# Tridiagonalising with the unscaled column: Householder steps reordered in an eigendecomposition kernel

## The reference

```
h = relu(layernorm(x));  x = x + L0(h)
h = relu(layernorm(x));  x = x + L1(h)

L0: deg = row sum + column sum - diagonal
    L_norm = D^-1/2 (diag(deg) - A) D^-1/2
    _, U = eigh(L_norm)
    agg = U^T h;  out = relu(agg W1 + b1) W2 + b2;  return U out
L1: two graph convolutions with adj, then LSTMs over windows of
    1, 2, 3 and 4 nodes, the last state written back
```

## Time and profile before

| | |
|---|---|
| median of three runs | 1360.0 us |
| profiled execution | 1349.57 us, span 1347.7 us |
| setup, to the first step | 0 to 8.4 us |
| tridiagonalisation | 8.4 to 342.8 us |
| eigenvalues and vectors | 343 to 497 us |
| L0 and L1 products | 497 to 1347.7 us |
| busy, share of the span | PE 93%, DVE 74%, ACT 68%, POOL 25% |

### The profile page before, as it was taken

One profiled execution on the slowest core, in us unless ns is written; L12 is line 12 of the kernel. 1 busy time (PEld: TensorE's weight loads), 2 busy tenths in 40 slices (PEclk: granted clock), 3 DMA queues, 4 the chain that ended last, 5 costly groups with the idle time before them and its releaser, 6 DMA issues.

```text
span 1347.7 us, 28362 instructions
## 1 busy us (share of the span) xinstructions
PE 1255.6 (93%) x8489; PEld 1124.5 (83%) x8489; DVE 991.2 (74%) x4880; ACT 917.3 (68%) x3438; POOL 331.7 (25%) x1205
## 2 busy tenths in 40 slices
PE   8889999999776379999999999999999999999997
PEld 7778888888665368788989989989989889899897
DVE  9999999999999977766774565655645655645645
ACT  4677777777599302267957858768579588578575
POOL 0288888888886010000110000000000000000000
PEclk9999999999789679999999999999999999999999
DMA  9500000000000003300010000100100100100001
GB/s 265 128 2 2 1 2 2 2 2 2 1 1 1 0 1 95 94 1 1 1 31 0 16 16 0 31 0 0 31 0 0 31 0 0 31 0 16 17 1 33
DMA packets 43642, 28.99 MB, mean 22 GB/s; under 512 B 1520, under 2 KB 39440, under 8 KB 43536
## 3 DMA queue, kind: packets, MB, share of 16 engines
q1 hardware_dynamic: 43536, 27.81, 7.6%
HBM read 19.42 MB, written 8.39 MB: 21 GB/s over the span
## 4 chain that ended last, share of the span: by engine, by line
PE 70%; DVE 20%; ACT 3%; issue 2%; ACTq 0%; DVEq 0%
PE bank L894 14%; PE bank L884 11%; PE bank L889 9%; PE bank L897 8%; PE bank L674 7%; PE bank L814 2%; PE bank L866 2%; PE bank L687 2%; PE bank L858 2%; PE bank L822 2%; PE bank L681 2%; PE bank L852 2%; PE bank L829 2%; PE bank L837 2%; ACT BIG L615 1%
## 5 line engine op out<-in xcount | busy, mean ns | idle before, releaser
L615 ACT ACTIVATE BIG<-bank,bias 128x128 f32<-128x128 f32 (+2 forms) x544 | 226.8, 417 | 161.6 <-PE bank L897 102.1
L894 PE MATMUL bank<-spare,wT 128*128 128x256 f32 (+2 forms) x1408 | 311.3, 321 | 0.0
L615 ACT ACTIVATE PV<-bank,bias 128x256 f32<-128x256 f32 (+2 forms) x704 | 301.6, 431 | 0.0
L894 PEld LDWEIGHTS bank<-spare,wT 128*128 128x128 f32 x1408 | 234.8, 191 | 13.2
L884 PE MATMUL bank<-spare,wT 128*128 128x128 f32 (+2 forms) x1088 | 226.3, 319 | 4.1 <-DVE spare L1610 2.7
L1596 DVE TENSOR_TENSOR BIG<-BIG,PV 128x128 f32<-128x128 f32 (+2 forms) x192 | 63.0, 328 | 207.5 <-ACT BIG L615 207.4
L674 PE MATMUL bank<-ones 128*128 128x128 f32 x1350 | 213.6, 291 | 1.1 <-POOL ones L313 1.1
L884 PEld LDWEIGHTS bank<-spare,wT 128*128 128x128 f32 x1088 | 169.5, 191 | 19.2 <-DVE spare L1610 6.1
L674 PEld LDWEIGHTS bank<-ones 128*128 128x128 f32 x1350 | 174.7, 195 | 1.1 <-POOL ones L313 1.1
L897 PE MATMUL bank<-spare,wT 128*128 128x128 f32 (+2 forms) x768 | 169.7, 303 | 0.0
L889 PE MATMUL bank<-spare,wT 128*128 128x128 f32 (+2 forms) x768 | 141.7, 307 | 3.7 <-DVE spare L1608 1.2
(11 more groups left out here) (478 smaller groups left out, 2670.5 us busy)
## 6 DMA issues: line engine op xcount, KB each, us to landing
spare<-in_x SPq DMA_DIRECT2D x32, 256.0 KB, 3.9
out<-X SPq DMA_DIRECT2D x32, 256.0 KB, 2.4
spare<-in_L_gnn_Wih SPq DMA_DIRECT2D x4, 256.0 KB, 4.5
spare<-in_L_gnn_Whh SPq DMA_DIRECT2D x4, 256.0 KB, 4.4
W<-in_L_gnn_W SPq DMA_DIRECT2D x2, 64.0 KB, 3.1
Wg<-in_L_gnn_Wg SPq DMA_DIRECT2D x2, 64.0 KB, 2.6
adj<-in_adj SPq DMA_DIRECT2D x1, 64.0 KB, 1.8
X<-in_x SPq DMA_DIRECT2D x4, 0.5 KB, 17.6
```

The lines of the kernel that those rows point to most:

```text
L615: last = nc.scalar.activation(gate_out[q][i][:, 0:T], gate(i, q, T), ACT.Tanh if q == GATE_G else ACT.Sigmoid, bias=bias[:, at:at + 1])
L894: last = nc.tensor.matmul(gate(i, q, T), wT[:, 0, p - 1, q * D:(q + 1) * D], xt, start=True, stop=(j == 0))
```

## The change

The reflector's scaled form is no longer computed before the product with A. With the column x unscaled, y = A x is multiplied at once, and u, its norm and the products with it are put together afterwards from x, y and A's column. `alpha` is the reciprocal of the signed norm, `eta` that of u's leading element, both kept for all steps in `invB`. Columns have a tiny constant added (`nudge`, 1e-10), which POOL makes at the start. The signs of stored quantities are turned.

The loop's part of the diff in short form: an arrow names the semaphore that an instruction raises, and VectorE's instructions stand as the arithmetic they do, one instruction for each assignment.

```diff
 # ScalarE, per step
-  two_sigma = Sqrt(4 x.x); half_x = Abs(x_t)/2; ST = Copy(x.x)
-  ACOL; row copy; eB = Identity(sign, scale=two_sigma); x_statistics (3 ops) once
+  act.wait_ge(s_ready, k + 1)
+  nc.scalar.activation(minus_sign(k), banks[7][:, 0:1], ACT.Sign)
+  nc.scalar.activation(sigma(k), banks[7][:, 1:2], ACT.Sqrt)
+  act.wait_ge(xb_ready, 2 * k + 1)
+  nc.scalar.activation(u_row(k)[:, t + 1:N], banks[0][:, t + 1:N], ACT.Copy)
+  act.wait_ge(hv, at_hv(k, MINUS_S))
+  nc.scalar.activation(S_(UC), ident[:, t:t + 1], ACT.Identity, bias=column(k), scale=rowsB[:, k:k + 1])
+  act.wait_ge(a_ready, k + 1)
+  nc.scalar.activation(S_(ACOL), A[:, t:t + 1], ACT.Copy, scale=below[:, t:t + 1])
+  statistic(2 * k)
+  act.wait_ge(xb_ready, 2 * k + 2); act.wait_ge(hv, at_hv(k, ETA))
+  nc.scalar.activation(eta_row[:, t + 1:N], banks[3][:, t + 1:N], ACT.Copy, scale=eta[:, t:t + 1])
+  statistic(2 * k + 1)
 # TensorE, per step
   pe.wait_ge(x_ready, k + 1)
   2-column product -> s_ready
-  row product; keep_clock(1); wait u_ready, a_ready; u row x A; A x u column; keep_clock(4)
+  nc.tensor.matmul(banks[0][:, 0:N], x_wide, ident[:, 0:N])   -> xb_ready
+  pe.wait_ge(taken, taken_by(k - 1, ETA_ROW))
+  nc.tensor.matmul(banks[3][:, 0:N], x_wide, minus_ident[:])  -> xb_ready
+  pe.wait_ge(a_ready, k + 1)
+  nc.tensor.matmul(banks[2][:, 0:N], x_wide, A[:])            -> yrow_ready
+  nc.tensor.matmul(banks[4][:, 0:1], A[:], x_c)               -> ycol_ready
+  pe.wait_ge(taken, taken_by(k, COL_U))
+  nc.tensor.matmul(banks[1][:, 0:N], S_(UC).to_broadcast([N, N]), A[:])  -> p_ready
+  idle(256)                        # one product of ones with 256 columns
 # VectorE, per step: 19 instructions (L1003 to L1057) replaced by 17
+  wait sigma_ready
+  minus_s = minus_sign * sigma;  minus_ut = minus_sign * sigma + x_t
+  alpha = 1 / minus_s;  eta = 1 / minus_ut;  XA = XM * alpha;  AM = below * alpha;  HX = XA * eta
+  wait taken (ROW), yrow_ready;  uyB = sum(y row * u row)       # wide
+  HXA = HX * alpha;  wait ycol_ready;  YA = y * AM + nudge
+  column(t) = HXA * uyB + YA       -> x_ready
+  wait p_ready;  Z = alpha * uyB + p_t;  wait taken (COLUMN);  W = YA + ACOL
+  A = p row * HX + A                                            # wide
+  V = HX * Z + W;  XM = column(t) * minus_below
+  wait taken (ETA_ROW);  A = eta_row * V + A  -> a_ready        # wide
```

More of the change, by code:

```diff
@@ L674, in keep_clock, with idle @@
                     nc.tensor.matmul(spot, ones[:], ones[:], start=True, stop=True)
+            def idle(columns):
+                if columns > 0:
+                    nc.tensor.matmul(banks[5][:, 0:columns], ones[:], ones[:, 0:1].to_broadcast([N, columns]),
+                                     start=True, stop=True)
             def householder(k):
+                t = k + 1
+                from_t = slice(t, N)
+                x_c = column(k)
+                x_wide = x_c.to_broadcast([N, N])
@@ new lines, in reflector @@
+                n_s = step(V.tensor_tensor(minus_s, minus_sign(k), sigma(k), ALU.mult))
+                n_ut = step(V.scalar_tensor_tensor(out=minus_ut, in0=minus_sign(k), scalar=sigma(k), in1=x_t,
+                                                   op0=ALU.mult, op1=ALU.add))
+                dve.wait_ge(hv, n_s)
+                n_al = step(V.reciprocal(alpha[:, t:t + 1], minus_s))
+                dve.wait_ge(hv, n_ut)
+                n_eta = step(V.reciprocal(eta[:, t:t + 1], minus_ut))
+                if not last:
+                    dve.wait_ge(hv, n_al)
+                    n_xa = step(V.tensor_tensor(S(XA), S(XM), alpha[:, t:t + 1], ALU.mult))
+                    n_am = step(V.tensor_tensor(S(AM), below[:, t:t + 1], alpha[:, t:t + 1], ALU.mult))
+                    dve.wait_ge(hv, n_xa)
+                    n_hx = step(V.tensor_tensor(S(HX), S(XA), eta[:, t:t + 1], ALU.mult))
+                    dve.wait_ge(taken, taken_by(k, ROW))
@@ new lines, in reflector @@
+                dve.wait_ge(yrow_ready, k + 2)
+                n_uy = step(V.tensor_tensor_reduce(out=wB[:, t:N], in0=banks[2][:, t:N], in1=u_row(k)[:, t:N], scale=1.0,
+                                                   scalar=0.0, op0=ALU.mult, op1=ALU.add, accum_out=uyB[:, t:t + 1]))
+                if last:
+                    return n_uy, None
+                dve.wait_ge(hv, n_hx)
+                step(V.tensor_tensor(S(HXA), S(HX), alpha[:, t:t + 1], ALU.mult))
+                dve.wait_ge(ycol_ready, k + 1)
@@ new lines, in diagonal @@
+            def diagonal(out, r, row, own):
+                h.last(dve)
+                op(V.tensor_tensor(row, alpha[r], uyB[r], ALU.mult))
+                op(V.tensor_tensor(own, wB[r], eta[r], ALU.mult))
+                op(V.tensor_tensor(row, row, own, ALU.subtract))
+                op(V.tensor_tensor(out, row, alpha[r], ALU.mult))
+            below_of(0)
+            for k in range(LEAF):
+                update(k, *reflector(k))
+            dve.wait_ge(taken, 1)
+            op(V.tensor_copy(d16[:, 0:1], dB[LP, 0:1]))
@@ L1073, in _ @@
             for k in range(LEAF, STEPS):
-                before = householder(k, before)
-            dve.wait_ge(e_ready, STEPS)
-            dve.wait_ge(a_ready, N)
+                n_uy, n_ya = reflector(k)
+                if k + 1 < STEPS:
+                    update(k, n_uy, n_ya)
             def go(ins):
```

278 lines of the change are left out of this document (137 added, 141 removed).

## The result

| | before | after |
|---|---|---|
| median | 1359.95 us | 1314.01 us |
| lowest and highest of four runs | 1351.77 to 1366.04 | 1313.11 to 1314.66 |
| profiled execution, its span | 1349.57, 1347.7 us | 1313.11, 1311.1 us |

The ratio is 0.9665, 95% interval 0.9614 to 0.9717: 46 us by the medians, 36.5 us by the two profiled executions. The profiled execution of before is not one of its four runs.

What follows compares the result with a forecast made beforehand. VectorE's in-order queue, taken as without holes, bounds the loop. 0.39 x 127 + 1 (diagonal) - 1 (X late) = 50, less 5 of POOL wait: 45 us off the 1360.0 median gives 1315 us, range 1302 to 1336.

Steps and rivals of the forecast that it cites:

- The step: Tridiagonalisation loop: a step falls from 2.63 to 2.24 us, saving 0.39 x 127 = 50 us.
- T+0.79: Start of A's second update, 0.79 us after T, the start of the VectorE instruction that writes the step's column.
- Just in time: In the loop step, the row A x is ready at S+0.65 (S: reflector start), exactly when VectorE reaches the dot product.
- ring: Loop path from A's second update through row product to dot product; row priced at T+1.65, equal to VectorE's queue.
- Rival B: Loop: ScalarE's or TensorE's queue late in every step, 2.40 us a step, gain 29, 1331 us; chance 0.20.
- The start and the diagonal: Once-only terms: X late for the statistics costs 1 us; dropping the diagonal's TensorE trip at step 16 gains 1.
- POOL: Leaf sweeps beside and behind the loop: end at about 435 us, VectorE's diagonal line then waits 5 us (bounds 0, 18).
- rival C: Behind the loop: POOL much later, an 18 us wait, gain 32, 1328 us; chance 0.07.
- A: Behind the loop: POOL is not last, gain 50 to 52, 1309 us; chance 0.15.
- D: Loop: Sign and Sqrt in different ScalarE tables, two loads a step, about 1635 us; chance 0.05.
- E: Loop: TensorE's clock falls to 1.2 GHz, steps up to 3.4 to 3.6 us, 1460 us; chance 0.04.
- Its own signs of being wrong: Four: table loads in the loop; clock below 1.00 before 290 us; VectorE idle before the reflector; POOL done well before diagonal.

Runs made afterwards that it cites:

- the XM run: Changed kernel with the masked-column instruction moved from before A's second update to behind it: 1315.5 us.
- the added copy: Changed kernel with one more one-column VectorE copy per step, right ahead of the dot product: 1313.6 us, 0.6 above the unedited kernel beside it.
- 17 sweeps: Changed kernel with 17 instead of 16 leaf QR sweeps on POOL: 1320.3 us; the same edit in the kernel before: ratio 0.9996.
- the dummies that removed it: Kernel before with one more 128 x 128 dummy product in each step from step 96 on: 1351.7 us.
- the kernel of 1432.7 us: Changed kernel with all four row products of a step narrowed to the live columns: 1432.7 us.

## Why the prediction was right, and where it was not

1. **The step.** Predicted 2.24 us, measured 2.33 as a mean, so 12 of the 50 us did not come. The structure was right in that all engines fit, A x comes just when the dot product asks for it, and the row product is the long link. It was wrong in what sets the step: the prediction took VectorE's queue to be without holes, and it has 2.6 us of them in 60. Two terms of the path through the row product were too small. I let A's second update start at T+0.79; it starts at T+0.86, because the dependent instruction comes 0.31 behind V, not 0.25 (the XM run shows the same 0.32 with nothing between them). And I let a reader on VectorE start 0.04 behind the end of a product, from the row of ScalarE (L493) in the earlier trace rows; L1059 starts 0.15 behind L733. With 0.03 more between the update and the product, and the part from the dot product to the next column 0.05 shorter than priced, that is 2.18 + 0.07 + 0.11 + 0.03 - 0.05 = 2.34, the step shown. "Just in time" was the place to look twice: where queue and ring are priced as equal, any error in the ring shows in full and one in the queue doesn't (the added copy: 0.6 us).
2. **Rival B** had 2.40 by late queues of ScalarE or TensorE. The size lies as near to B as to the forecast; the cause isn't B's. In the step shown TensorE and ScalarE both wait 0.38 us for VectorE's column and its product, and in every step of the profile but the one at half clock TensorE's first product (L726) starts 0.27 to 0.32 us behind the column: its queue is not late.
3. **The statistics** beside VectorE's steps: nothing, as predicted (0.1%, within the error).
4. **The start and the diagonal.** ScalarE waits 0.84 us for X and VectorE 0.21 for that: under the 1 us taken. At the leaf break a step takes 1.45 us more than its neighbours, before it took 2.72 more (by the starts of L1079, and of L1047 before): 1.3 us gained. In this execution half clock behind TensorE's gap takes 1.0 us of that back in the next step; in the second profile of the changed kernel 1.75 us over three steps, with 17 sweeps nothing. The gap isn't new (1.41 us, before 1.37), but the prediction had priced neither it nor the clock behind it.
5. **POOL.** Predicted to end its sweeps at about 435 us: 434.3. Errors cancel in that. POOL starts 4.5 us earlier, not 7 (first instruction at 51.42 instead of 55.92 us), and less of its work moves behind the loop, which ends 38 us earlier and not 50. The wait of 5 us isn't there, since VectorE came 12 us later than predicted; there is a slack of about 13 us instead, and 12 of them are the loop's shortfall. The balance of a few us that the prediction saw was therefore there. So rival C is out, and A holds in its premise (POOL isn't last) but not in its gain. The hope that the new loop, whose first update reads PSUM, would hold POOL up less did not show: a sweep in it takes (300.68 - 75.88)/10 = 22.5 us, as before.
6. **D and E.** Sign and Sqrt stand one behind the other 127 times with one table load in the program. The clock is 1.00 in the loop but for the leaf break. E's price of a step was right (3.41 us) and its danger real: three edited kernels fell into it.
7. **The sum.** 38 us for the loop instead of 50, no wait of POOL instead of 5: against the profiled execution 1349.6 - 45 = 1304.6 was predicted and 1313.1 came, 8.5 us off. The forecast of 1315 fits because I took the same 45 off the median, 10.4 us above that execution. Those 10 us are not a constant offset, as I had treated them: they come of the clock falling at the end of the old loop in about half of its executions (seen in two profiles of 1373 and 1375 us, inferred for the group at 1360 from the dummies that removed it), and no profile of the new loop shows that fall. So the median gained 10 us that no step of my sum contained, and they cover the 8.5. That the total was right to 1 us is in this part luck, all the more as the median of before moves between 1352 and 1366 us from call to call. Over equal clocks the change is worth 36.5 us.
8. **Its own signs of being wrong.** Two of the four that the prediction named came true although the time fitted: the clock was below 1.00 before 290 us (0.83 from 50 to 60), and POOL was done well before the diagonal line. Of what it expected to see, VectorE without holes is not there, and the dot product starts 0.15 and not 0.1 us behind its row.

## What to carry to other kernels

Where a new loop is priced and two paths come out equal, price the ring once more with every "result to dependent reader" measured for that pair of engines, since the ring has no slack to hide an error in. If the runs of a kernel stand in groups, compare the granted clock of the groups before taking a difference off the median. And look at the granted clock behind every gap on TensorE, even one of 1.4 us: here it was nearly the same gap before and after, and the fall behind it cost from nothing to over 100 us, depending on the kernel and on the execution. Five dummy products in it kept the clock up in the one kernel where they were tried.

## What was not expected of the hardware

- TensorE's clock stood at 0.50 for 370 us with TensorE busy 98.6 to 100% of each window (the kernel of 1432.7 us), with steps of 3.41 us. In kernels that differ from it only in product widths, dummies or POOL's sweeps it did not fall in the loop at all, came back after one to three steps, after 14, or not before the loop's end.
- The fall stood behind 1.4 us without a product in 7 of 8 profiled executions of the changed kernel and its edits, and in 1 of 5 of the old one with nearly the same gap; five dummy products of 128 columns in the gap removed it, with six executions within 0.6 us.
- In the step shown a product of 2 columns is followed by the next after 0.24 us, and one of 128 columns after 0.31 to 0.33: narrowing one product by half on the mean gained 0.05 us.
- From the end of a product to its reader: 0.04 us to ScalarE, 0.15 us to VectorE's dot product.
